# Transformer layer, last token block: six rows of h kept, the down products done tile by tile, and the branch one unit later

## What is computed

```python
x = layernorm(x + attention(x))
g = (x @ gate_w.T) * gate_s
u = (x @ up_w.T) * up_s
x = layernorm(x + ((silu(g) * u) @ down_w.T) * down_s)
```

## Time and profile before

| | us |
|---|---|
| runs | 1103.7, 1103.6, 1101.34 (median 1103.6) |
| profiled execution | 1103.08 |
| its span | 1101.3 |
| TensorE busy | 1049.2 (95%) |
| VectorE busy | 783.8 (71%) |
| ScalarE busy | 637.8 (58%) |
| GpSimd busy | 249.8 (23%) |

### The profile page before, as it was taken

The page is one execution under the profiler, slowest core; times in us unless marked ns, Lnnn a source line. Parts: engine busy times, 40 slices in busy tenths (PEclk is TensorE's granted clock), DMA queues, the critical chain, the costliest instruction groups (busy, mean ns, idle before and its releaser), DMA issues.

```text
span 1101.3 us, 14972 instructions
## 1 busy us (share of the span) xinstructions
PE 1049.2 (95%) x5732; PEld 546.4 (50%) x5732; DVE 783.8 (71%) x892; ACT 637.8 (58%) x1205; POOL 249.8 (23%) x215
## 2 busy tenths in 40 slices
PE   8999999999999999999999999999899999999995
PEld 3533334433444433443444433333346688888784
DVE  5789968899779799779788899999413435362534
ACT  2158866778677788778666688878651022322221
POOL 1151030442331531245210144552001100000002
PEclk9999999999999999999999999999999999999998
DMA  6074416243242521433142445411215201010011
GB/s 231 39 186 125 103 35 204 51 94 84 52 111 71 94 74 40 86 97 94 33 74 50 140 98 161 117 59 48 98 49 126 76 21 39 1 39 1 1 39 40
DMA packets 36732, 87.49 MB, mean 79 GB/s; under 512 B 12528, under 2 KB 12912, under 8 KB 34448
## 3 DMA queue, kind: packets, MB, share of 16 engines
q1 hardware_dynamic: 36080, 85.76, 29.0%
q10 hardware_dynamic: 576, 0.72, 0.2%
HBM read 49.76 MB, written 23.86 MB: 67 GB/s over the span
## 4 chain that ended last, share of the span: by engine, by line
PE 64%; ACT 11%; DVE 2%; issue 1%; DMA 1%; POOL 0%; SPq 0%; DVEq 0%; POOLq 0%
PE PV L564 18%; PE PS L544 16%; PE PSA L1124 14%; ACT Bn L550 9%; PE PS L1169 5%; PE PS L269 3%; PE PSA L683 2%; PE PS L683 2%; PE PV L1169 2%; ACT Bn L580 1%; PE PSA L472 1%; DVE nmx L483 1%; DMA wr<-A 1%; PE PSA L1069 1%; ACT A L347 0%
## 5 line engine op out<-in xcount | busy, mean ns | idle before, releaser
L483 DVE TENSOR_REDUCE nmx<-PSA 128x1 f32<-128x1024 f32 x512 | 599.8, 1217 | 91.0 <-PE PSA L472 90.9
L550 ACT ACTIVATE Bn<-PS 128x512 f32<-128x512 f32 x1024 | 529.0, 605 | 150.8 <-PE PS L544 150.1
L544 PE MATMUL PS<-Qt,Kt 50*128 50x512 f32 x1024 | 373.8, 446 | 30.8 <-ACT Bn L550 17.7
L472 PE MATMUL PSA<-Kt,Qt 48*128 48x512 f32 x1024 | 393.7, 463 | 2.7 <-DVE nmx L483 1.7
L544 PEld LDWEIGHTS PS<-Qt,Kt 50*128 50x128 f32 x1024 | 167.3, 184 | 327.6 <-ACT Bn L550 298.0
L564 PE MATMUL PV<-Bn 128*32 128x512 f32 x2048 | 272.8, 605 | 0.0
L472 PEld LDWEIGHTS PSA<-Kt,Qt 48*128 48x128 f32 x1024 | 166.0, 184 | 33.3 <-DVE nmx L483 15.2
L1124 PE MATMUL PSA<-x1Th,wr 128*128 128x512 f32 x344 | 136.1, 396 | 1.2 <-DMA wr<-A 0.7
L1124 PE MATMUL PSA<-x1Tl,wr 128*128 128x512 f32 x344 | 134.8, 392 | 0.0
L1144 DVE SCALAR_TENSOR_TENSOR sg<-PSA,us,sg 128x512 f32<-128x512 f32 x43 | 32.1, 748 | 131.7 <-ACT sg L1135 131.6
L1135 ACT ACTIVATE sg<-PSA,gs 128x512 f32<-128x512 f32 x43 | 29.5, 689 | 157.2 <-PE PSA L1124 157.2
(11 more groups left out here) (137 smaller groups left out, 751.8 us busy)
## 6 DMA issues: line engine op xcount, KB each, us to landing
Qt<-pscr SPq DMA_DIRECT2D x90, 128.0 KB, 4.7
A<-in_wf SPq DMA_DIRECT2D x11, 768.0 KB, 6.6
wr<-A SPq DMA_DIRECT2D x33, 256.0 KB, 2.7
pscr<-A SPq DMA_DIRECT2D x16, 512.0 KB, 3.7
vscr<-Bn SPq DMA_DIRECT2D x32, 256.0 KB, 2.0
Kt<-pscr SPq DMA_DIRECT2D x90, 64.0 KB, 2.4
A<-in_xT SPq DMA_DIRECT2D x4, 1024.0 KB, 7.4
A<-A SPq DMA_DIRECT2D x16, 256.0 KB, 3.7
```

The source lines that it names most:

```text
L472: r = pe.do(lambda e, h=h, p=p: e.matmul(ps[:, h, :], Qt[i][p:p + NC_, g % 2, 128 * qt:128 * qt + 128], Kt[i][p:p + NC_, 512 * h:512 * h + ...
L483: r_mxs[hh, s] = dve.do(lambda e: e.tensor_reduce(nmx[:, hh % 2, c0:c0 + 1], ps, AX.XY, ALU.max, negate=True), c_rel[s])
L544: r = pe.do(lambda e: e.matmul(PS2[:, c % 3, :], Kt[i][rows, 128 * kt:128 * kt + 128], Qt[i][rows, g % 2, 512 * qh:512 * qh + 512], start= ...
L550: r_exp[c] = act.do(lambda e: e.activation(Pb[c % NP_], PS2[:, c % 3, :], ACT.Exp, scale=0.25), c_exp)
```

## The change

It has three parts.
- Rows 38 to 43 of h (`held` = 44 - 6 = 38) go to six pairs of buffers of their own, `hTz`. Four lie where the input parts of the third token block were, two in the place of weight rows that have been copied elsewhere by then. `down` runs inside the loop only up to row 37, so that gate and up of rows 39 to 43 follow each other.
- `last_norm` does the 48 down products of rows 38 to 43 (i = 5 to 10) by tiles: rows 5 to 9 of tile 0, rows 5 to 9 of tile 1, row 10 of both, then all six rows of tile 2 and of tile 3. In the list behind it `measure` of tile 2 comes before `scale` of tile 3, and `store` of tile 1 after `measure` of tile 3.
- `SPLIT` is U - 12 in place of U - 13: unit 243, and the turn of maxima in it, stands ahead of the branch.

```diff
--- before.py
+++ after.py
@@ -973,7 +973,7 @@
             put(n, w, lambda: next(look))
 
         U = 16 * NG
-        SPLIT = U - 13
+        SPLIT = U - 12
 
         def unit(u, fill=None):
 
@@ -1029,6 +1029,9 @@
         hTx = [[at(f"hT{p}{i}", 2048 * (2 * i + j), [128, 512], F32R) for j, p in enumerate("hl")] for i in range(2)]
         x1Tx = [[at(f"x1T{p}{n}", o + 8192 * j, [128, KT, 512], F32R) for j, p in enumerate("hl")]
                 for n, o in enumerate((12288, 32 * ((base_a + 8223) // 32) - base))]
+        KEPT = 6
+        hTz = [[at(f"hz{p}{i}", (12288 + 4096 * i if i < 4 else in_a(12800 + 1024 * (i - 4))) + 2048 * j, [128, 512], F32R)
+                for j, p in enumerate("hl")] for i in range(KEPT)]
         wplace = ([32768, 34816, 10240] + [53248, 55296, 30720] + [74368, 76416, 78464] + [80512, 94848]
                   + [36864 + 2048 * j for j in range(8)] + [57344 + 2048 * j for j in range(4)]
                   + [66176 + 2048 * j for j in range(4)] + [82560 + 2048 * j for j in range(6)])
@@ -1050,6 +1053,10 @@
 
 
             r_xt, r_h, r_dn, r_zf, r_gu = {}, {}, {}, {}, {}
+            held = 4 * FI - (KEPT if exact else 2)
+
+            def h_parts(q):
+                return hTx[q % 2] if q < held else hTz[q - held]
             r_zd = [(), ()]
             r_bank = {}
             if exact:
@@ -1136,7 +1143,7 @@
                 dve.wait(r, r_late["us"])
                 dve.wait(*(() if exact else free_b))
                 if exact:
-                    hf, (hi, lo) = sg[q % 2], hTx[q % 2]
+                    hf, (hi, lo) = sg[q % 2], h_parts(q)
                 else:
                     hf = hTf[q % 3]
                     if q >= 3:
@@ -1148,8 +1155,10 @@
                 r_h[q] = r
                 if exact:
                     if q >= 2:
-                        act.wait(r_dn[q - 2])
-                        dve.wait(r_dn[q - 2])
+                        free_h = [r_dn[q - 2]] if q < held else [r_gu[2], r_pj[1], *(r_wr[8, p] for p in range(2)),
+                                                                 *(r_wr[9, p] for p in range(2))]
+                        act.wait(*free_h)
+                        dve.wait(*free_h)
                     act.wait(r)
                     r = act.do(lambda e: e.copy(hi[:, :], hf), c_hh)
                     dve.wait(r)
@@ -1161,7 +1170,7 @@
                 pe.wait(r_h[q])
                 if exact:
                     pe.wait(r_wr[i, 1])
-                    pairs = [(h[:, 128 * t:128 * t + 128], wr[i][2][:, :]) for h in hTx[q % 2]]
+                    pairs = [(h[:, 128 * t:128 * t + 128], wr[i][2][:, :]) for h in h_parts(q)]
                 else:
                     pairs = [(hTf[q % 3][:, 128 * t:128 * t + 128], wf[:, i, 2, :])]
                 for m, (h, w) in enumerate(pairs):
@@ -1207,7 +1216,9 @@
             def last_norm():
 
                 got = {}
-                for t, i in ((0, 9), (1, 9), (2, 9), (0, 10), (1, 10), (3, 9), (2, 10), (3, 10)):
+                rows = range(held - 3 * FI, FI) if exact else (9, 10)
+                order = [(t, i) for t in range(2) for i in rows[:-1]] + [(t, FI - 1) for t in range(2)]
+                for t, i in order + [(t, i) for t in (2, 3) for i in rows]:
                     got[t] = down_tile(3, i, t, c_dn)
                 r_dn[3 * FI + FI - 1] = got[3]
                 dve.wait(r_late["ds"], *last_ln)
@@ -1240,7 +1251,7 @@
                     sp.do(lambda e: e.dma_start(out_d[t0:t0 + 128, :], zz[t]), c_out[t // 2], 16)
 
                 for f, t in ((scale, 0), (scale, 1), (measure, 0), (scale, 2), (measure, 1), (store, 0),
-                             (scale, 3), (measure, 2), (store, 1), (measure, 3), (store, 2), (store, 3)):
+                             (measure, 2), (scale, 3), (measure, 3), (store, 1), (store, 2), (store, 3)):
                     f(t)
 
             ahead = []
@@ -1290,13 +1301,7 @@
                 ahead[:2] = []
             for q in range(2 if exact else 0, 4 * FI + 1):
                 tb, i = divmod(q, FI)
-                if exact and q == 4 * FI - 1:
-                    last = gate_up(tb, i)
-                    for _ in range(17):
-                        next(last)
-                    down(*divmod(q - 2, FI))
-                    whole(last)
-                elif q < 4 * FI:
+                if q < 4 * FI:
                     whole(ahead.pop(0) if ahead else gate_up(tb, i))
                 if norm is not None and 1 <= i < FI - 1:
                     next(norm, None)
@@ -1310,7 +1315,7 @@
                                 copy_weights(i2, part)
                 if i in turns_at and tb < 3:
                     turn_x1(tb + 1, turns_at.index(i))
-                if 1 <= q < 4 * FI - 1 - (1 if exact else 0):
+                if 1 <= q <= held:
                     down(*divmod(q - 1, FI))
                     if i == 0:
                         norm = second_norm(tb - 1)
```

## The result

| | before | after |
|---|---|---|
| runs, us | 1101.34 to 1103.7, median 1102.24 (6) | 1097.41 to 1100.38, median 1098.57 (6) |
| profiled execution, us | 1103.08 | 1099.4 |
| its span, us | 1101.3 | 1097.6 |
| span from the last usable product to the end ("tail"), us | 11.94 | 8.00 |

The ratio of the runs is 0.9959, with a 95% interval of 0.9942 to 0.9976: 0.41% faster, about 4.5 us with an interval of 2.6 to 6.4 us, clear of no change. The medians of the table differ by less, 3.67 us, which lies inside that interval.

The account below looks back on a forecast made before the run. TensorE was taken to bound the kernel up to its last product, then the chain behind it. The span's end moves from 1101.3 to 1093.8 + 2.98 + 0.1 = 1096.9, 4.4 us earlier; from the median 1103.6, forecast 1099.2, range 1096.6 to 1102.0.

Parts of the forecast that it names:

- the wait for row 43: On TensorE among the last down products: the 0.28 us gap goes, with 1.4 us of cover to spare.
- The products: On TensorE: number and 0.232 us pitch unchanged, no waits for banks or new buffers, last product starting at 1088.60.
- Tile 3 late by 0.72 us: On VectorE behind the last product: tile 2 is measured from 1089.0, tile 3 scaled only at 1089.8, 0.72 us late.
- The chain of tile 3, 4.00 us: Tile 3 from scaling and add through statistics and small operations to final scaling: 4.00 us, VectorE ending at 1093.8.
- The last leg, 3.08 us: From VectorE's end to the program's end: 2.98 us of DMA and closing as before, plus 0.1 for crowded stores.
- The sum: The tail behind the last product: TensorE idle for about 7.8 us, not 11.9.
- The moved branch at nothing: Branch one attention unit later, SyncE's order changed: costs nothing, between a gain of 0.4 and a loss of 2.0 us.
- Rival 1: At the moved branch: an instruction fetch of 2.0 to 2.7 us leaves 2.0 us gain, 1101.6; chance 0.11.
- Rival 2: In the tail: VectorE's order holds tile 3 and three stores crowd, gain 2.2 to 3.3 us, about 1100.8; chance 0.08.
- Rival 3: In the tail: tile 3 not late and the maxima's earlier return helps, gain over 5.2 us, about 1098; chance 0.07.
- Rival 4: At the 48 last down products: TensorE pauses, clock halves, 11.1 us more, 1110.3; chance 0.06.
- The signs: In the profile: tile 2's scaling 2.5 us before tile 3's, stores within 1.6 us; wrong if tile 3 over 1.5 late.

Follow-up runs that it names:

- e9: The changed kernel itself measured once more, with no edit; ratio to the kernel before 0.9971 (0.9959 to 0.9983).
- e2: The change with its last down products row by row over the four tiles and the old list of norm and store steps; ratio to the kernel before 1.0016.
- e5: The change with four rows kept in place of six; one execution, 311.11 us from first gate product to end, 313.33 in the kernel before.
- e7: The change with the final scalings of tiles 0 to 2 on ScalarE in place of VectorE; ratio to the kernel before 0.9969.
- e4: The change with the old list of norm and store steps; one execution, 308.56 us from first gate product to end, 313.33 in the kernel before.
- e1: The change with the branch put back to its old unit (SPLIT = U - 13); ratio to the kernel before 0.9965.
- e6: The change with eight rows kept in place of six, also waiting for the copies of weight row 10; ratio to the kernel before 0.9952.
- e3: The change with two rows kept in place of six and row 41's down products as cover; ratio to the kernel before 1.0009.
- e8: The change with eight rows kept, final scalings of tiles 0 to 2 on ScalarE and the epsilon addition on VectorE; ratio to the kernel before 0.9953.
- e10: The kernel with eight rows, ScalarE final scalings and VectorE epsilon addition measured again, beside the change; ratio to the kernel before 0.9950.

## Why the prediction was right

The forecast was a gain of 4.4 us and 1099.2; measured were 1098.57 and a ratio that stands for 4.5 us, inside the range. That the time itself came within 0.6 us is in part luck: the forecast was counted from a median of 1103.6, that of the six runs was 1102.24, and the medians differ by 3.67 us. The firmer check is the profile, where what the change does adds up to 4.2 us (3.94 of tail and 0.28 of wait). Between the two profiled executions the span lost 3.7 us. It is made of: tail 3.94; the wait for row 43, 0.28; the wait for a copied row, 0.47 less by chance; together 4.69, or 4.73 as counted from the first gate product. Against that stand 1.03 us that the changed kernel's profile was late at that product already, before anything that the change touches: its clock was 0.97 over the first 50 us, where that of the kernel before was 1.00. e9, the same kernel at 1.00 over that stretch, reached the first gate product at 787.50, 1.50 us earlier than this execution.

- *The products*: right. No wait for banks, none for row 43, none at row 38's new buffers, and the pitch stayed (0.2315 against 0.232). e2 and e5 show the 0.28 us for what it is, give or take 0.1.
- *Tile 3 late by 0.72 us*: measured 0.44. The collision of tile 0's final scaling with GpSimd's add was there, but the scaling ended at 1089.30, 0.29 us behind the add as expected; the add itself was 0.3 us earlier relative to the last product than I had put it. The reason is the first small operation of tile 0 ahead of it: I took 0.54 us from a row in which VectorE's final scaling ran beside it, and it took 0.31 to the next (0.23 by itself). Of the 0.44 the collision accounts for 0.17, since e7, which has none, is late by 0.27 from waiting for the add alone; I had put 0.3 on it.
- *The chain of tile 3, 4.00 us*: measured 4.21 (1090.04 to 1094.25). Two terms were too small by 0.1 us each. From aggregation to final scaling it was 1.52 us where the sum has 0.27 + 0.54 + 0.60 = 1.41, since two final scalings of VectorE now run beside the small operations and slow the second of them too. I had said that these scalings fit in the time in which GpSimd has the values; they do, but without them it takes 1.17, as e7 shows. And from tile 3's scaling to its statistics it was 1.42 where I took 1.32 from the earlier trace rows: there the statistics behind tile 3's add are those of tile 2 (the list before has `measure` of tile 2 there), which needn't wait for that add.
- *The last leg, 3.08 us*: measured 3.35. I took 0.1 us for crowding, out of 0 to 0.7; it is 0.37. e4 and e7, with stores 1.3 us apart, have 2.97 and 2.79.
- *The sum*: 7.8 us of tail forecast, 8.00 measured. The three errors are -0.28, +0.21 and +0.27; that the sum is off by no more than 0.2 is luck too, as they partly cancel.
- *The moved branch at nothing*: right, by e1 and by the 20.03 to 20.07 us of the three. The bound of 0.4 us of gain was not there to be had: the 0.37 us gap is not the branch's. The DMA order changed as forecast, with the copies issued from 778.80 (777.8 forecast; this execution was 1.05 us late at L950), and no one waited for them. Rival 1, the fetch, would have shown as a stop of 2 us; there is none. No run here shows what a taken branch to code far away costs.
- *Rival 2* (worse tail) had both its mechanisms in it, at 0.44 and 0.37 us rather than 1 to 2. *Rival 3* needed tile 3 not to be late, which e6 gives with two more rows. *Rival 4*: TensorE never paused, and its clock was 1.00 up to 1089.6.
- *The signs*: tile 2's scaling stood 3.27 us before tile 3's, the last final scaling ended 4.65 us after the last product was usable, the three last stores were issued within 1.45 us, and TensorE was idle for 8.00 us; none of the signs of being wrong appeared.

What the gain rests on is the distance between tile 0 and tile 3 on TensorE, compared with the 6.5 us or so that VectorE and GpSimd need from the scaling of tile 0 (1083.58) until they are free for tile 3 (1090.04). Two rows kept give 2.3 us of that distance, six give 6.0 and eight 7.9: six fall short by the 0.44 us that tile 3 is late, eight have enough (VectorE then stood idle 0.52 us before tile 3's scaling), and what is left to win behind the last product then lies in tile 3's own chain and the last leg.

## What to carry to other kernels

At the end of a program, what counts is not how soon the last product comes but how much of the work behind it can be done before. Keep the operands of the last steps and finish one output tile after another; the number to keep follows from what the engines behind need for all tiles but the last, here 6.5 us, divided by what each kept row gives, here 0.93 us; that makes seven rows, which was not run. When the last tile is alone, look at what still runs beside its chain: two operations that "fit in the gap" of another engine cost 0.35 us here, and three stores within 1.45 us cost 0.3 to 0.6 us.

## What was not expected of the hardware

**VectorE's scaling slows GpSimd even at 128x1.** A GpSimd operation on one column took 0.42 us while VectorE's final scaling of 128x512 ran, and 0.22 without; the power took 0.71 and 0.56. The same two engines meet in the final scaling of tile 0: 1.10 us beside GpSimd's add in the change, 0.55 alone. ScalarE did the same scaling in 0.82 us beside an add of GpSimd that kept its 1.29. The Trainium skill (SBUF — State Buffer, "SBUF: two separate sides") has this as an exclusive lock on a port pair shared by VectorE and GpSimd, with ports of its own for ScalarE. The traces agree that either engine holds up the other, and that ScalarE is spared; they don't agree with a full block in every case. The final scaling of tile 0 ended 0.29 us after GpSimd's add, although it takes 0.55 alone. And VectorE's add of tile 3, which has two inputs in SBUF, took its usual 0.69 us from 1090.73 on, beside GpSimd's power, which kept its 0.56:

```profile
1090.51 0.56 POOL L1242 TENSOR_TENSOR ve<-ve,half 128x1 f32<-128x1 f32 x1
```

**The spread of runs goes with the clock, and the lower stretches lie early.** The kernel before took 1101.87 us at a mean clock of 0.997 and 1108.04 at 0.990 (26 runs beside e1 to e4, and those between lie on that line within 1.4 us). Where tails differ, mean clocks can't be compared as they stand: the mean takes in the idle tail, where the granted clock was 0.61 before and 0.78 after. The windows from 200 to 250 us of e2, one of the two slowest profiles, and of the kernel before:

```profile
200.00:250.00 50.00, 47.48 (x278) 17.75 (x280) 42.38 (x41) 36.49 (x71) 23.69 (x22) 0.90 0.34 78
```

```profile
200.00:250.00 50.00, 47.23 (x300) 18.69 (x293) 45.95 (x44) 39.11 (x77) 27.07 (x25) 1.00 0.33 77
```

The clock has two levels, 1.2 and 2.4 GHz, so a mean of 0.90 over 50 us is 10 us at the lower one; in e2 they lie from 222 to 232 us, where TensorE had been busy for 20.3 of the 22 us before. e2 reached its first gate product at 791.89, 3.9 us after the kernel before, in a part where the kernels are the same but for the branch. In the profiled executions all stretches at the lower level ahead of the tail lie before 250 us, but for the one of e3 at 790. What brings them about stays open. That is why differences of 1 us had to be read from the profiles' tails, which repeat to 0.01 us between e1, e9 and the change and to 0.15 between e8 and e10, and not from the runs.
